# A new order of all queues for the first nine tiles of a fused quantized product and LoRA kernel

## The chip, the cores and the metric

The kernel runs on one core of a Trainium2 chip. The metric is the time of one execution on the device, in microseconds (us). A core has four compute engines with a queue of instructions each, worked off in order: TensorE (PE; its weight loads are shown apart as PEld), VectorE (DVE), ScalarE (ACT) and GpSimd (POOL). A fifth queue, SP, only issues DMAs here. Engines wait for each other by semaphores; an instruction that waits holds up all behind it in its queue.

## What is computed

x has 2 batches of 1024 rows of 2048 numbers, ctx 2 batches of 2048 x 2048. Cut to what matters:

```python
def fake_quant(x, scale, zp):
    q = clip(round(x / scale + zp), 0, 255)
    return (q - zp) * scale

# first stage
x = x + tanh(g_xattn) * (fake_quant(layernorm(x)) @ fake_quant(ctx))
# second stage, on h = layernorm(x)
logits = h @ Wr.T                        # 4 experts
gates = softmax(top 2 of logits)         # 0 for the others
mid = einsum('tf,erf->ter', h, A)        # rank 16
delta = sum_e gates_e * (mid_e @ B_e.T) * 4
out = x + tanh(g_ffn) * delta
```

## The kernel before

**Tiles and stages.** The 2048 rows of x are 16 tiles (b) of 128 rows; tiles 0 to 7 belong to batch 0, tiles 8 to 15 to batch 1. A tile lies in one of five buffers (`xr`, RING = 5), where x1, the delta and the output are made in place: tile 5 can be loaded only when tile 0 is stored. ctx is cut into 64 "rows" (i) of 128 x 1024 fp32, 0.52 MB each; 0 to 31 are batch 0 (16 blocks k of its left half, then 16 of its right half), 32 to 63 batch 1. A row is loaded to a staging place, scaled to bytes by ACT (`scale_row`, line 446), and made an fp16 code in `q2` by DVE (`code_row`, line 1139). Two byte buffers stand between the two.

**The first stage of tile b**: `stats_x` in two halves, `var_x`, `power_x` on POOL (line 376), `scale_of_x`, then ACT's `scale_x` (452), 8 transposes of PE (`turn_q1`, 654), and the copy to `q1T` (`copy_q1T`, DVE for tiles 0 and 1, ACT after, 460). The product is 4 column blocks n x 16 blocks k of 128x512 matmuls (671). For tiles 0 to 3 it is issued by halves and k, as the rows come (`rows(b, half, first, end)`, two matmuls for each k); from tile 4 on by column block (`main(b, n, first, end)`). `add_main` (DVE, 1200) adds a column block to x.

**The second stage of tile b**: `stats_h` for each column block (1205), `var_h`, `power_h` on POOL (381), `bias_h`; ACT's `high_part` (470, fp16 part of the normalized row) and `normal_half` (476, the fp32 value, by halves); POOL's `low_part` (390, their difference, two instructions for each half). PE turns the parts, 8 transposes for each half (`turn_hi` 708, `turn_lo` 715), ACT and DVE copy them out (`copy_hiT` 482, `copy_loT` 487 on ACT for half 0, 1223 on DVE for half 1), PE multiplies them with A (`mid_hi` 727, `mid_lo` 735, 8 matmuls each). DVE ranks the gates (`rank_gates`), ACT takes `gate_exp` (491), DVE `weigh` (last instruction 1257), PE `turn_gate` (746), DVE `split_gate` (1265, 1267), PE `delta` (754, 756, two matmuls for each of 4 column blocks), DVE `add_delta` (1273), SP `store`.

**The order.** Each engine's block is a list of such steps, written out by hand for the first nine tiles (0 to 8); from STEADY = 9 on it is a loop that staggers the stages of neighbouring tiles. Every step waits for what it needs, for instance:

```python
def low_part(b, h):
    pool.wait_ge(h2_ready, 2 * b + h + 1)
    pool.wait_ge(h_hi_ready, b + 1)
    wait(pool, lo_turned, 2 * (b - 1) + h + 1)
def load_x(b, h):
    wait(sp, out_stored[b % RING], 32 * (b // RING))
def turn_lo(b, h):
    pe.wait_ge(h_lo_ready, 4 * b + 2 * h + 2)
    pe.wait_ge(hiT_ready, 2 * b + h + 1)
```

Once, early, A is loaded and split (`largest_of_a`, `powers_of_a`, `copy_scales` on DVE, `scales_of_a` and `spread_scales` on PE, `split_a` on POOL, three instructions) and B likewise (`high_of_b`, `low_of_b` on DVE). `keep_busy(n)` is n matmuls whose result is not used. Rows 48 to 63 are staged in places that earlier rows leave, one of them `q1T`'s fourth buffer.

Of the kernel before, what the change touches and what calls it, by code (L numbers as in the profile page):

```python
# [34 lines left out]
def build(nc, x, ctx_in, params, lora_a, lora_b, out):  # L35
# [21 lines left out]
    with ExitStack() as stack:  # L57
# [188 lines left out]
        def _(sp):  # L246
# [34 lines left out]
            load_x(2, 0)  # L281
            load_x(2, 1)
            load_row(4)
            load_row(5)
            load_x(3, 0)
            load_x(3, 1)
            for i in range(6, 16):
                load_row(i)
            load_a()
            for i in range(16, 20):  # L290
                load_row(i)
            load_b()
            for i in range(20, 32):
                load_row(i)
            load_x(4, 0)
            load_x(4, 1)
            for i in range(32, 48):
                load_row(i)
            store(0, 0)
            load_row(48)  # L300
            store(0, 1)
            load_x(5, 0)
            load_x(5, 1)
            load_row(49)
            store(1, 0)
            load_row(50)
            load_row(51)
            store(1, 1)
            load_x(6, 0)
            load_x(6, 1)  # L310
            load_row(52)
            load_row(53)
            store(2, 0)
            store(2, 1)
            load_x(7, 0)
            load_x(7, 1)
            store(3, 0)
            load_row(54)
            store(3, 1)
            load_row(55)  # L320
            load_row(56)
            load_x(8, 0)
            load_x(8, 1)
            load_row(57)
            store(4, 0)
            load_row(58)
            store(4, 1)
            load_row(59)
            load_x(9, 0)
            load_x(9, 1)  # L330
            load_row(60)
            load_row(61)
            load_row(62)
            store(5, 0)
            load_row(63)
            store(5, 1)
            load_x(10, 0)
            load_x(10, 1)
            store(6, 0)
            store(6, 1)  # L340
# [18 lines left out]
        def _(pool):  # L359
# [54 lines left out]
            low_part(4, 0)  # L414
            power_x(6)
            low_part(4, 1)
            power_h(5)
            power_x(7)
            low_part(5, 0)
            low_part(5, 1)  # L420
            power_x(8)
            power_x(9)
            for b in range(6, 8):
                power_h(b)
                low_part(b, 0)
                low_part(b, 1)
# [10 lines left out]
        def _(act):  # L437
# [55 lines left out]
            scale_row(0)  # L493
            scale_x(0)
            scale_row(1)
            scale_row(2)
            scale_row(3)
            scale_row(4)
            scale_x(1)
            scale_row(5)  # L500
            scale_row(6)
            scale_x(2)
            scale_row(7)
            scale_row(8)
            copy_q1T(2)
            scale_row(9)
            scale_x(3)
            scale_row(10)
            scale_row(11)
            copy_q1T(3)  # L510
            for i in range(12, 30):
                scale_row(i)
            scale_x(4)
            for i in range(30, 35):
                scale_row(i)
            copy_q1T(4)
# [54 lines left out]
            for i in range(50, 56):  # L571
                scale_row(i)
# [1034 lines left out]
```

## Time and profile before

| | us |
|---|---|
| median of 3 runs (lowest, highest) | 376.11 (375.16, 376.32) |
| profiled execution, its own time | 376.49 |
| its span | 374.7 |
| PE busy | 337.6 (90%) |
| DVE busy | 290.2 (77%) |
| ACT busy | 251.0 (67%) |
| POOL busy | 96.8 (26%) |
| mean granted clock of PE | 0.982 |

The span runs from the first to the last instruction of the profiled execution; the run's own time has 1.8 us more around it. A row of the timeline names start, duration, engine, line and operation, output<-input and the number of instructions merged in it; in brackets stand the idle time before it and what ended that. A matmul is listed for longer than it holds up the next one, so starts, not durations, tell PE's pace. The granted clock is the share of 2.4 GHz that PE got; it is either 1.00 or 0.50 (1.2 GHz), and a mean between them is a mixture.

### The profile page before, as it was taken

The page shows a single profiled execution, that of the slowest core. Times are in us where ns is not written, and L with a number is a line of the kernel's source. Part 1 is how long each engine was busy: PE and PEld are TensorE (multiplying, and loading weights), DVE is VectorE, ACT ScalarE, POOL GpSimd, SP SyncE. Part 2 cuts the span into 40 slices and gives each one's busy share as a digit, 9 for nine tenths or more (in the row PEclk, how much of TensorE's full clock was granted, in tenths as well). Part 3 has the DMA queues.
Part 4 walks back from the last instruction along what each step waited for, and adds up shares of the span by engine and source line. Part 5 has one row for each costly group of instructions (what it writes and reads, how often), then busy time and mean ns, then how long its engine had stood idle before and what let it go on. Part 6 is the DMA issues. An engine that isn't in the chain of part 4 may idle for free. (4 is left out here: it accounts for less than half of the span.)

```text
span 374.7 us, 6441 instructions
## 1 busy us (share of the span) xinstructions
PE 337.6 (90%) x2372; PEld 188.7 (50%) x2372; DVE 290.2 (77%) x715; ACT 251.0 (67%) x207; POOL 96.8 (26%) x107
## 2 busy tenths in 40 slices
PE   0579989999985789999989999999999999999984
PEld 0234434445653665455555556464656565555552
DVE  4785889589996799999947796968686877866685
ACT  1769848949999699689898147464747473756150
POOL 3100430005545322033043222140505050505000
PEclk9999999999998599999999999999999999999999
DMA  7999999960046769672570524141405020202023
GB/s 218 415 420 419 420 420 420 417 278 2 3 148 239 268 247 359 213 260 87 172 258 1 193 107 152 56 170 57 170 34 192 2 115 1 114 0 114 0 86 140
DMA packets 19185, 69.17 MB, mean 185 GB/s; under 512 B 2256, under 2 KB 2256, under 8 KB 19024
## 3 DMA queue, kind: packets, MB, share of 16 engines
q1 hardware_dynamic: 19152, 68.73, 48.4%
q8 instruction: 21, 0.34, 0.4%
q14 instruction: 12, 0.10, 0.1%
HBM read 51.94 MB, written 16.78 MB: 183 GB/s over the span
## 5 line engine op out<-in xcount | busy, mean ns | idle before, releaser
L671 PE MATMUL ps_main<-q,q1T 128*128 128x512 f16 x832 | 197.4, 379 | 2.2 <-ACT q1T L460 1.6
L671 PEld LDWEIGHTS ps_main<-q,q1T 128*128 128x128 f16 x832 | 77.4, 98 | 87.2 <-issue 9.0
L446 ACT ACTIVATE c_code<-q,small_tile 128x1024 uint8<-128x1024 f32 x62 | 74.7, 1239 | 25.0 <-DVE q L1139 13.7
L470 ACT ACTIVATE h_parts<-xr,small_tile 128x2048 f16<-128x2048 f32 x15 | 31.4, 2094 | 39.4 <-DVE small_tile L1217 39.4
L390 POOL TENSOR_TENSOR h_parts<-work,h_parts 128x512 f16<-128x512 f32 x30 | 34.8, 1180 | 66.3 <-ACT work L476 66.3
L1139 DVE TENSOR_SCALAR q<-c_code,small_tile 128x1024 f16<-128x1024 f16 x64 | 37.0, 580 | 14.0 <-ACT c_code L446 13.6
L1200 DVE SCALAR_TENSOR_TENSOR xr<-ps_main,small_tile,xr 128x512 f32<-128x512 f32 x52 | 38.6, 743 | 8.1 <-PE ps_main L671 8.0
L1144 DVE BATCH_NORM_STATS2 small_tile<-xr 128x6 f32<-128x512 f32 x64 | 40.9, 680 | 5.2 <-DMA xr<-in_x 5.2
L1205 DVE BATCH_NORM_STATS2 small_tile<-xr 128x6 f32<-128x512 f32 x64 | 43.6, 687 | 0.9
L1273 DVE TENSOR_TENSOR xr<-ps_delta,xr 128x512 f32<-128x512 f32 x62 | 41.2, 680 | 3.9 <-PE ps_delta L756 3.2
L381 POOL TENSOR_TENSOR small_tile<-small_tile 128x1 f32<-128x1 f32 x16 | 9.3, 583 | 128.3 <-DVE small_tile L1213 128.3
L482 ACT COPY hT<-ps_turn 128x1024 f16<-128x1024 f16 x32 | 31.4, 1006 | 12.5 <-PE ps_turn L708 12.4
L452 ACT ACTIVATE x_byte<-xr,small_tile 128x2048 uint8<-128x2048 f32 x16 | 33.5, 2092 | 7.8 <-DVE small_tile L1159 7.8
L390 POOL TENSOR_TENSOR h_parts<-q1T,h_parts 128x512 f16<-128x512 f32 x30 | 34.1, 1160 | 1.3 <-ACT q1T L476 1.3
L754 PE MATMUL ps_delta<-lora_bT,gT_hi 128*128 128x512 f32 x60 | 30.1, 502 | 0.4 <-DVE gT_hi L1265 0.3
L460 ACT ACTIVATE q1T<-ps_gate,small_tile 128x2048 f16<-128x2048 uint8 x12 | 23.6, 1964 | 8.0 <-PE ps_gate L654 8.0
L756 PE MATMUL ps_delta<-lora_bT,gT_lo 128*128 128x512 f32 x60 | 24.4, 406 | 0.0
L642 PE MATMUL ps_main<-ident_h 128*128 128x512 f16 x47 | 12.9, 421 | 12.2 <-issue 12.2
L376 POOL TENSOR_TENSOR small_tile<-small_tile 128x1 f32<-128x1 f32 x16 | 9.5, 595 | 53.7 <-DVE small_tile L1151 53.7
L1223 DVE COPY hT<-ps_turn 128x1024 f16<-128x1024 f16 x16 | 11.0, 687 | 15.4 <-PE ps_turn L715 15.4
L671 PE MATMUL ps_turn<-q,q1T 128*128 128x512 f16 x64 | 18.1, 380 | 4.8 <-DVE q L1139 3.1
L727 PE MATMUL ps_mid<-a_parts,hT 128*128 128x136 f16 x256 | 20.8, 229 | 0.9 <-ACT hT L482 0.9
(122 smaller groups left out, 415.1 us busy)
## 6 DMA issues: line engine op xcount, KB each, us to landing
q<-in_ctx SPq DMA_DIRECT2D x62, 512.0 KB, 10.9
xr<-in_x SPq DMA_DIRECT2D x32, 512.0 KB, 4.9
out_x<-xr SPq DMA_DIRECT2D x30, 512.0 KB, 3.4
h_parts<-in_B SPq DMA_DIRECT2D x1, 1024.0 KB, 16.5
q1T<-in_ctx SPq DMA_DIRECT2D x2, 512.0 KB, 6.4
out_x<-xr SPq DMA_DIRECT2D x4, 256.0 KB, 2.3
xr<-in_A SPq DMA_DIRECT2D x1, 544.0 KB, 16.2
small_tile<-in_params SPq DMA_DIRECT2D x1, 3.0 KB, 2.6
```

The source lines that it names most:

```text
L390: nc.gpsimd.tensor_tensor(h_lo[:, half(h)][:, part], work[h][:, part], h_hi[:, half(h)][:, part], ALU.subtract).then_inc(h_lo_ready, 1)
L446: nc.scalar.activation(c_byte[:, i % 2, :], stage(i), ACT.Identity, bias=par[:, 3:4], scale=inv_s[:, 1:2]).then_inc(row_scaled, 1)
L452: nc.scalar.activation(x_byte[:, :], xr[:, b % RING, :], ACT.Identity, bias=q_scale[:, 1:2], scale=q_scale[:, 0:1]).then_inc(x_scaled, 1)
L470: nc.scalar.activation(h_hi[:, :], xr[:, b % RING, :], ACT.Identity, bias=h_bias[:, b % 2:b % 2 + 1], scale=h_rstd[:, b % 2:b % 2 + 1]).th ...
L482: nc.scalar.copy(hT[:, h, :, :], as16(ps_turn[h], F16).rearrange("p (k m) -> p k m", m=P)).then_inc(hiT_ready, 1)
L671: mm = pe.matmul(product_bank(b, n)[:, :], q1T_of(b)[:, k, :], q2[:, batch(b), k, cols(n)], start=(k == 0), stop=(k == KT - 1))
L754: pe.matmul(ps_delta[n % 2][:, :], gT_hi[:, :], lora_bT[:, cols(n)], start=True, stop=False)
L1139: nc.vector.tensor_scalar(q2[:, batch_of, k, half(h)], c_code[:, i % 2, :], low_centre[:, :], None, ALU.add).then_inc(row_coded, 1)
L1144: nc.vector.bn_stats(x_stats[:, n, :], xr[:, b % RING, cols(n)]).then_inc(x_stats_done, 1)
L1200: nc.vector.scalar_tensor_tensor(out=x1, in0=product_bank(b, n)[:, :], scalar=gain[:, 0:1], in1=x1, op0=ALU.mult, op1=ALU.add).then_inc(x1 ...
L1205: nc.vector.bn_stats(h_stats[:, b % 2, n, :], xr[:, b % RING, cols(n)]).then_inc(h_stats_done, 1)
L1273: nc.vector.tensor_tensor(x1, src[:, :], x1, ALU.add).then_inc(out_ready, 1)
```

## The change

All five lists for tiles 0 to 8 are written in another order; the loop from tile 9 on stays, and so do all steps: none is added, removed or altered. Only `rows` and `main` calls are cut at other k.

- **PE:** the halves of tiles 0 to 3 are mixed more finely: the right half (`rows(b, 1, ...)`) of tiles 0 and 1 starts before the left half of tile 3 ends. `turn_q1(1)` and `turn_q1(2)` come earlier against tile 0's products, `keep_busy(8)` stands behind `turn_q1(2)`. The second stage of tile 0 starts within tile 3's products, and the steps of tiles 1 to 3 are spread over tiles 4 and 5.
- **DVE:** `high_of_b` moves from behind row 13 to behind row 15 and `add_main(0, 0)`, `low_of_b` from behind row 14 to behind row 25; `largest_of_a` stands behind row 8; `stats_x(3)` behind row 9; rows 63 and 62 come later.
- **ACT:** `scale_x(4)` moves from behind row 29 to behind row 35, `copy_q1T(4)` behind `copy_hiT(0, 0)`, `copy_q1T(5)` behind `copy_hiT(3, 1)`.
- **POOL:** `power_x(5)` moves from behind `low_part(3, ...)` to ahead of it; `power_h(1)` behind `low_part(0, ...)`.
- **SP:** rows 5 to 9 are loaded before tile 3's x, A between its halves, B behind row 17 instead of 19; rows and stores from 47 on are mixed otherwise: `store(2, 1)` before `store(2, 0)`, `store(5, 1)` and `store(6, 0)` before `store(5, 0)`.

From the diff, the place between tile 4's last products and tile 5's first on PE, and POOL's list:

```diff
             power_h(0)
-            for b in range(1, 5):
+            low_part(0, 0)
+            low_part(0, 1)
+            power_h(1)
+            for b in range(2, 4):
                 power_h(b)
                 low_part(b - 1, 0)
                 low_part(b - 1, 1)
-            power_x(5)
...
+            for b in range(5, 7):
+                power_x(b)
+                low_part(b - 2, 0)
+                low_part(b - 2, 1)
+                power_h(b - 1)
...
-                mid_hi(3, 1)
-                turn_lo(3, 1)
-                delta(2, 0)
-                delta(2, 1)
...
+                main(4, 3, general, 9, 11)
                 delta(1, 3)
-                turn_hi(3, 0)
-                mid_lo(2, 1)
-                turn_hi(3, 1)
+                main(4, 3, general, 11, 12)
                 turn_lo(3, 0)
+                main(4, 3, general, 12, 16)
                 turn_gate(2, 5)
```

**PE, between tile 1's last deltas and tile 5's first product.** `ps_main<-q,q1T` (L671) is a product, `ps_turn<-ident_h,h_parts` a turn of a high (L708) or low (L715) part, `ps_mid` a mid_hi (L727) or mid_lo (L735), L746 a turn_gate, `ps_delta` a delta (L754 and L756). Before:

```order
479 L754 MATMUL ps_delta<-lora_bT,gT_hi 128x512
480 L756 MATMUL ps_delta<-lora_bT,gT_lo 128x512
481 L708 MATMUL ps_turn<-ident_h,h_parts 128x128 x8
482 L735 MATMUL ps_mid<-a_parts,hT 128x68 x8
483 L708 MATMUL ps_turn<-ident_h,h_parts 128x128 x8
484 L715 MATMUL ps_turn<-ident_h,h_parts 128x128 x8
485 L746 MATMUL ps_gate<-ident_f,gated 128x128
486 L727 MATMUL ps_mid<-a_parts,hT 128x136 x16
487 L715 MATMUL ps_turn<-ident_h,h_parts 128x128 x8
```

and after, where tile 3's parts are turned:

```order
477 L708 MATMUL ps_turn<-ident_h,h_parts 128x128 x8
478 L671 MATMUL ps_main<-q,q1T 128x512
479 L754 MATMUL ps_delta<-lora_bT,gT_hi 128x512
480 L756 MATMUL ps_delta<-lora_bT,gT_lo 128x512
481 L671 MATMUL ps_main<-q,q1T 128x512 x2
482 L708 MATMUL ps_turn<-ident_h,h_parts 128x128 x8
483 L735 MATMUL ps_mid<-a_parts,hT 128x68 x8
484 L671 MATMUL ps_main<-q,q1T 128x512 x2
485 L754 MATMUL ps_delta<-lora_bT,gT_hi 128x512
486 L756 MATMUL ps_delta<-lora_bT,gT_lo 128x512
487 L671 MATMUL ps_main<-q,q1T 128x512
488 L715 MATMUL ps_turn<-ident_h,h_parts 128x128 x8
```

Between the same short steps there now stand products of tile 4's last column block.

**POOL, around tile 3's low part.** L376 is a power_x, L381 a power_h (L374 and L379 in the changed file), L390 a low_part (L388). Before:

```order
28 L390 TENSOR_TENSOR h_parts<-q1T,h_parts 128x512 x2
29 L381 TENSOR_TENSOR small_tile<-small_tile 128x1
30 L390 TENSOR_TENSOR h_parts<-work,h_parts 128x512 x2
31 L390 TENSOR_TENSOR h_parts<-q1T,h_parts 128x512 x2
32 L376 TENSOR_TENSOR small_tile<-small_tile 128x1
```

After:

```order
28 L388 TENSOR_TENSOR h_parts<-q1T,h_parts 128x512 x2
29 L374 TENSOR_TENSOR small_tile<-small_tile 128x1
30 L388 TENSOR_TENSOR h_parts<-work,h_parts 128x512 x2
31 L388 TENSOR_TENSOR h_parts<-q1T,h_parts 128x512 x2
32 L379 TENSOR_TENSOR small_tile<-small_tile 128x1
```

power_x(5), row 32 before, is row 29 now, ahead of low_part(3, 0), row 30.

## Rows read from the trace of the kernel before

**Rows 1.** The page, part 1: busy us (share of the span) and instructions.
```profile
PE 337.6 (90%) x2372; PEld 188.7 (50%) x2372; DVE 290.2 (77%) x715; ACT 251.0 (67%) x207; POOL 96.8 (26%) x107
```

**Rows 2.** Stretches of the span; columns as in its first line.
```profile
core 0: us, PE busy (x) PEld busy (x) DVE busy (x) ACT busy (x) POOL busy (x), PEclk, DMA share, GB/s
12.00:86.60 74.60, 67.54 (x326) 29.97 (x326) 58.64 (x106) 56.62 (x43) 10.00 (x8) 1.00 0.95 388
86.60:108.00 21.40, 21.18 (x199) 13.40 (x200) 19.97 (x49) 21.40 (x21) 11.26 (x11) 1.00 0.04 15
108.00:118.00 10.00, 8.20 (x79) 5.28 (x76) 7.75 (x25) 10.00 (x10) 5.42 (x5) 1.00 0.69 205
118.00:137.00 19.00, 11.47 (x101) 9.58 (x102) 15.51 (x49) 15.28 (x15) 5.22 (x5) 0.64 0.76 292
137.00:216.00 79.00, 77.62 (x563) 43.43 (x562) 65.15 (x170) 62.83 (x53) 22.23 (x23) 1.00 0.55 193
216.00:374.70 158.70, 151.56 (x1112) 87.04 (x1109) 117.66 (x296) 81.65 (x67) 38.99 (x42) 1.00 0.23 88
```

**Rows 3.** Timeline of PE, 86 to 137: start, duration, engine, line, operation.
```profile
86.61 0.61 PE L671 MATMUL ps_main<-q,q1T 128*128 128x512 f16 x2 [0.63 <-DVE xr L1200]
...
87.95 2.54 PE L671 MATMUL ps_main<-q,q1T 128*128 128x512 f16 x11
90.32 0.64 PE L727 MATMUL ps_mid<-a_parts,hT 128*128 128x136 f16 x8
90.80 1.03 PE L671 MATMUL ps_main<-q,q1T 128*128 128x512 f16 x4
...
107.39 0.41 PE L735 MATMUL ps_mid<-a_parts,hT 128*128 128x68 f16 x8
107.64 1.06 PE L708 MATMUL ps_turn<-ident_h,h_parts 128*128 128x128 f16 x16
108.53 2.10 PE L671 MATMUL ps_main<-q,q1T 128*128 128x512 f16 x9
...
136.29 1.24 PE L671 MATMUL ps_main<-q,q1T 128*128 128x512 f16 x5 [1.26 <-ACT q1T L460]
```

**Rows 4.** PE's waits, 80 to 140: total us, times, longest.
```profile
PE ps_mid L735 <- DVE hT L1223: 3.8, 1, 3.8
PE ps_gate L746 <- DVE gated L1257: 2.5, 1, 2.5
```

**Rows 5.** Timeline of PE, two rows in tile 7.
```profile
181.12 1.04 PE L671 MATMUL ps_main<-q,q1T 128*128 128x512 f16 x4
...
182.47 0.82 PE L671 MATMUL ps_main<-q,q1T 128*128 128x512 f16 x3
```

**Rows 6.** Timeline of PE, where it waits for row 14's code.
```profile
50.09 0.61 PE L671 MATMUL ps_turn<-q,q1T 128*128 128x512 f16 x2 [1.66 <-DVE q L1139]
```

**Rows 7.** Timeline of DVE: row 14's code.
```profile
47.56 2.48 DVE L1139 TENSOR_SCALAR q<-c_code,small_tile 128x1024 f16<-128x1024 f16 x1
```

**Rows 8.** Timeline of DVE, 102 to 120.
```profile
102.74 1.48 DVE L1139 TENSOR_SCALAR q<-c_code,small_tile 128x1024 f16<-128x1024 f16 x1 [0.37 <-ACT c_code L446]
104.15 0.68 DVE L1273 TENSOR_TENSOR xr<-ps_delta,xr 128x512 f32<-128x512 f32 x1
104.75 0.47 DVE L1139 TENSOR_SCALAR q<-c_code,small_tile 128x1024 f16<-128x1024 f16 x1
...
119.25 1.28 DVE L1144 BATCH_NORM_STATS2 small_tile<-xr 128x6 f32<-128x512 f32 x2 [3.16 <-DMA xr<-in_x]
```

**Rows 9.** Timeline of the DMA queue SP: issues.
```profile
108.42 0.34 SPq L270 DMA_DIRECT2D out_x<-xr  x1
114.05 0.81 SPq L251 DMA_DIRECT2D xr<-in_x  x2
```

**Rows 10.** Timeline of POOL: half a low part.
```profile
119.63 2.27 POOL L390 TENSOR_TENSOR h_parts<-work,h_parts 128x512 f16<-128x512 f32 x2 [4.45 <-ACT work L476]
```

**Rows 11.** Groups of DVE, 80 to 216: count, busy us, mean ns, idle before.
```profile
L1139 DVE TENSOR_SCALAR q<-c_code,small_tile 128x1024 f16<-128x1024 f16 x31 | 17.7, 569 | 6.3 <-ACT c_code L446 6.2
```

More of the change, by code:

```diff
@@ L1337, in _ @@
-            stats_x(4, 1)
-            code_row(26)
-            var_x(4)
-            code_row(27)
-            scale_of_x(4)
-            for i in range(28, 33):
-                code_row(i)
+            code_row(33)
             add_main(0, 2)
+            stats_h(0, 2)
             add_main(0, 3)
-            stats_h(0, 2)
+            code_row(34)
+            stats_h(0, 3)
+            var_h(0)
+            stats_h(1, 0)
+            bias_h(0)
             add_main(1, 2)
-            stats_h(0, 3)
+            stats_h(1, 1)
@@ L1378, in _ @@
             var_h(3)
-            rank_gates(0)
-            code_row(37)
+            add_delta(0, 0)
+            bias_h(2)
+            add_delta(0, 1)
+            code_row(38)
+            add_delta(0, 2)
+            add_main(4, 0)
+            add_delta(0, 3)
+            copy_loT(1)
+            code_row(39)
+            bias_h(3)
+            code_row(40)
+            rank_gates(1)
+            stats_h(4, 0)
+            weigh(1)
             add_main(4, 1)
-            weigh(0)
-            stats_h(4, 0)
+            code_row(41)
@@ L1461, in _ @@
+            code_row(53)
             var_h(5)
-            add_delta(4, 3)
-            code_row(53)
             add_main(6, 0)
             bias_h(5)
+            rank_gates(4)
+            add_main(6, 1)
+            var_x(7)
             code_row(54)
-            var_x(7)
+            weigh(4)
+            scale_of_x(7)
+            stats_x(8, 0)
+            split_gate(4)
+            add_main(6, 2)
+            stats_x(8, 1)
+            stats_h(6, 0)
+            var_x(8)
+            add_delta(4, 0)
@@ L1478, in _ @@
+            copy_loT(5)
+            bias_h(6)
+            code_row(57)
+            code_row(58)
+            add_main(7, 0)
+            rank_gates(5)
+            add_main(7, 1)
+            weigh(5)
+            code_row(59)
+            split_gate(5)
             stats_x(9, 0)
-            stats_h(6, 2)
-            scale_of_x(8)
-            copy_loT(5)
             stats_x(9, 1)
-            code_row(57)
-            rank_gates(5)
-            add_main(6, 3)
+            add_main(7, 2)
@@ L1486, in _ @@
+            stats_h(7, 0)
             var_x(9)
-            weigh(5)
-            code_row(58)
-            stats_h(6, 3)
-            split_gate(5)
-            add_main(7, 0)
-            code_row(59)
-            var_h(6)
             add_delta(5, 0)
+            stats_h(7, 1)
+            scale_of_x(9)
             code_row(60)
+            add_main(7, 3)
+            stats_h(7, 2)
+            code_row(61)
+            stats_h(7, 3)
+            var_h(7)
+            copy_loT(6)
+            bias_h(7)
@@ L1508, in _ @@
-            code_row(63)
-            copy_loT(6)
-            add_main(7, 3)
-            stats_h(7, 3)
-            rank_gates(6)
-            var_h(7)
-            bias_h(7)
-            weigh(6)
-            add_main(8, 0)
-            stats_h(8, 0)
-            split_gate(6)
             add_delta(6, 0)
             add_delta(6, 1)
+            stats_h(8, 1)
             add_delta(6, 2)
-            add_main(8, 1)
-            add_delta(6, 3)
-            stats_h(8, 1)
             copy_loT(7)
+            code_row(63)
```

786 lines of the change are left out of this document (390 added, 396 removed).

## The prediction

> **What bounds the kernel now.** I first read the page's shares: TensorE (PE) is busy for 337.6 of 374.7 us and no other engine passes 77%, so PE's queue sets the time, and the question is where PE loses [rows 1]. The stretches, read next, put numbers on that [rows 2]. At about 216.0 PE comes to tile 9's first product, and from there the program is unchanged, so what follows is taken as a block of 158.7 us. Ahead of it PE is idle for 7.1 us of 12 to 86.6, for 0.2 us of 86.6 to 108, for 1.8 us of 108 to 118, for 7.5 us of 118 to 137 (where the granted clock averages 0.64), and for 1.4 us of 137 to 216.
>
> The timeline shows what stands in the gap [rows 3]. Tile 4's product begins at 86.61, its last 9 matmuls start at 108.53, and the first matmul of tile 5's starts at 136.29. Between them PE has nothing but short steps of the second stage of tiles 1 to 4, and each depends on an answer from ScalarE (ACT), VectorE (DVE) or GpSimd (POOL). The list of waits names the two longest: 3.8 us for DVE's copy of the turned low part and 2.5 us for the gate weights [rows 4]. After PE had been idle for 3.8 us, matmuls ran at the 1.2 GHz level: a mean of 0.64 over 19 us is 13.7 us at that level.
>
> **The method.** No instruction is added or taken away, the 25 warming matmuls included, so PE's work to tile 9 is the same and only waits and the clock can move. From pieces that run without a wait I take PE's steps, as the distance to the next start: 0.216 us for a product matmul (87.95 to 90.32 is 11), 0.45 for 8 transposes (107.64 to 108.53 is 16), 0.47 for a mid_hi, 0.25 for a mid_lo [rows 3], 0.47 for a delta of two matmuls (181.12 to 182.47 is four products and one, 0.49; others were 0.47) [rows 5], and an estimated 0.13 for a turn_gate, a single matmul. I add them along the new order and ask at each wait whether the thing waited for is there.
>
> **Part A, the first half tiles.** Before, the tightest row was row 14: PE reached it, without waiting, at 27.9 us of its own work, and waited until 50.1 [rows 6], a lag of 22.1 us behind its work. The row was late since high_of_b stands ahead of it on DVE, up to 47.56, and since it was coded beside POOL's split_a, in 2.48 us [rows 7] where one undisturbed takes 0.47 [rows 8]. The new order puts high_of_b and low_of_b behind rows 15 and 25, but calls rows 14 and 15 at 21.0 and 22.7 us of work. Walked through: q1T(1) is made behind row 6, x tile 2 is coded for turn_q1(2) at about 27.2, the 8 warming matmuls end at 29.4, which is a lag of 19.6, and spread_scales ends near 39. Then rows 14 and 15 are coded beside split_a, by 41.5 and 44.0 at 2.2 and 2.5 us each: a lag of 21.3 at row 15. That is 0.8 less than 22.1, and the wait of 0.6 us for a free bank at tile 4 [rows 3] goes, as add_main(3,2) falls 0.8 us ahead of its reader. Sum 1.4; I count **1.0**. The order of the loads costs nothing: rows 5 to 9 come one to two places earlier, x tile 3 and A later, and at 388 GB/s or more [rows 2] a place of 0.52 MB is at most 1.35 us; row 31 still lands near 60 and PE calls it at 69.
>
> **Part B, tile 4's start to tile 5's start.** Before: 86.61 to 136.29, 49.7 us [rows 3]. By the steps above its work is 34.2 us (64 product matmuls 13.8, 19 groups of 8 transposes 8.6, 8 mid_hi 3.8, 8 mid_lo 2.0, 12 deltas 5.6, 3 gates 0.4), so 15.5 us are waits, half clock and the fills behind each wait. In the new order PE has 66.0 us of work to tile 4's first product, which at a lag of 21.3 is 87.3, and 30.0 us from there to tile 5's (the same 64 products and 12 deltas, but 13 groups of transposes, 6 mid_hi and 6 mid_lo). In it the steps of tile 0 stand in tile 3's products, and those of tiles 2 and 3 in tile 4's and 5's. Only nine short groups, 3.9 us, are left between tile 4's last product matmul and tile 5's first. I find three waits there:
> - turn_hi(3,0) meets high_part(3), which ACT ends 0.6 us late.
> - turn_lo(3,0) needs POOL's low_part(3,0), and POOL now has power_x(5) ahead of it. That chain starts at DVE's add_delta(0,3): PE's turn_gate(0) comes at 92.2, and from there DVE has split_gate, stats_h, var_h, add_delta, bias_h, add_delta, a code row, add_delta, add_main and add_delta, 5.1 us at the steps of its rows (0.60 us from start to start for one over 512 columns, 0.39 for a code row [rows 8]), so with a wait or two it ends near 97.6. Then the store, 5.6 us until the buffer's load is issued, as 108.42 to 114.05 before, and 5.2 us to the statistics, as 114.05 to 119.25 [rows 8, 9]. That gives 108.4; with stats_x, code rows, copy_loT, stats_x and var_x on DVE 112.6, power_x 0.6 and low_part 2.27 [rows 10] 115.5. PE comes near 113.1: 2.2 us, and 2.5 us more for PE if that load lands that much later.
> - copy_hiT(3,1) stands behind scale_x(5) and a row on ACT: 0.3 us.
>
> These are 3.1 us, plus 0.5 for fills: tile 5 starts at 87.3 + 30.0 + 3.6 = 120.9. None reaches the 3.8 us pause behind which the clock fell. So B gives 15.5 - 3.6 = **11.9**.
>
> **Part C, tiles 5 to 8.** Before PE idles 1.4 us here. Walked on with PE at a lag of 24.4, the tightest meetings are scale_x(7), 1 us ahead of turn_q1(7), code_row(62), 0.9 us ahead of its matmul, and rank_gates(7), whose weights come 1.0 us ahead of turn_gate(7). Stores and loads on SP: x tile 8 waits behind row 57 and lands at about the time DVE asks, x tile 9 some 0.8 us late, x tile 10 (behind store(5,1), store(6,0) and store(5,0)) near 204, as the loop asks for it; DVE absorbs these. C gives **1.0**.
>
> **What eats some of it.** After 80 us DVE's 31 code rows take a mean of 569 ns [rows 11], where an undisturbed one takes 470 [rows 8]: 3.1 us of stretching that my walk, at 470, leaves out. Most is covered, since in the walk DVE waits for PE for some 4.5 us between tiles 5 and 9, so I take **0.4**; its bounds are 0 and 3.1 (nothing covered).
>
> Sum: 1.0 + 11.9 + 1.0 - 0.4 = 13.5. The profiled execution took 376.49 us (span 374.7 and 1.8 around it), so 363.0; the median of the runs lies 0.4 lower, so **362.6 us**.
>
> **A rule weighed.** From 86.6 to 108 PE ran 199 matmuls, 80 of them transposes, among products, as the new order does everywhere, and the granted clock was 1.00 [rows 2]; 8 of them took 0.45 us [rows 3]. The Trainium skill (TensorE: Matmul & The Clock Gate, Part 4) has it that transposes don't count as work that holds the clock up. By that rule the clock could fall where steps are spread, and the sum would be that of the second rival; this trace, with 40% of transposes at a clock of 1.00, does not bear it out.
>
> **The rivals.**
> 1. *The gap is only moved, 12%.* From 86.6 to 108 ACT is busy for all of 21.4 us and DVE for 20.0 [rows 2], and the new order asks them for the same work in 13 us less. If at each of tiles 5 to 9 PE waits 1.2 us for ACT's or DVE's lateness, 6 us come back: 369. For it: margins of 1 us. Against: from 137 to 216 DVE is busy for 65 of 79 us, so it can catch up.
> 2. *The clock falls once more, 5%.* PE now waits up to 2.5 us for turn_q1(2) near 25 us, right after warming, and 1.9 us before that. A stretch of 13.7 us at 1.2 GHz, as before, costs 6.9 us under full load: 369.5. The same price holds if the fall comes among the spread transposes. Against: before, the clock stayed up through every wait but that of 3.8 us [rows 2, 4].
> 3. *Slower, 4%: the code rows meet POOL.* Rows 36 to 63 are 28 rows. If each falls beside a low_part and takes 1.48 us [rows 8], DVE has 28.3 us more; less the 3.1 that it had before and the 4.5 us of slack, PE is 20.7 us later: 383. The Trainium skill (GPSIMD Engine Reference, Specifications) says that this engine shares its SBUF interfaces with VectorE and contends with its instructions in a two-port mode; the rows agree, with 2.48 us at worst [rows 7]. It turns the sign once 18 rows are hit (18 x 1.01 = 13.5 + 4.5). Against: their mean was 569 ns [rows 11], and POOL's 16 low parts of 2.27 us fill a third of the stretch.
> 4. *Nothing changes, 2%:* the spread steps free no time as main(5,0) waits for q1T(5) anyway: copy_q1T(5) would have to end at 136 instead of 121. Its chain hangs on the same load of x tile 5, which starts with add_delta(0,3), 10 us earlier; against it. 376.
>
> **How the numbers follow.** The forecast as worked out has 77%. Within it the bounds are A from -2 (turn_q1(2) later) to +2, the load of x tile 5 from 2.2 us better to 5 us worse, stretching 0 to 3.1. All together would give 358 to 372; the ends that are likely together are 360 and 367. Rivals 1 and 2 lie at 369, and the range reaches to them: **359.5 to 369.5**, with rivals 3, 4 and the far corners outside. Differences over 0.3% (1.1 us) count as a change, about what a measurement of this kernel can tell. Faster 0.94, same 0.02, slower 0.04.
>
> **What would show it.** Tile 4's first product at 87 to 89 and tile 5's at 121 (118 to 124); no granted clock below 1.00 between 17 and 340 us; DVE's wait for x tile 5 near 108; tile 9's first product at 202 to 203. If tile 5 starts by 122 and tile 9 only after 207, rival 1 is right. A granted clock of 0.5 after 17 us is rival 2. Code rows at a mean above 0.8 us are rival 3. If tile 5's first product waits for q1T beyond 130, rival 4. The prediction is wrong if any stretch of PE's idle time above 3 us is left between 52 and 200.

## The result, and the profile after

The changed kernel takes 359.43 us (median of 4 runs, 358.62 to 361.46) beside 376.22 us of the kernel before (4 runs, 375.16 to 376.65): a ratio of 0.956, with a 95% interval of 0.952 to 0.960. It is faster by 16.8 us where 13.5 were forecast. The profiled execution took 361.46 us, the slowest of the four, beside 376.49 before: 15.0 us less. Two executions among the experiments below, one of e1 (896.73 us) and one of e9 (367.23 us), were slow runs and stand outside all medians and ratios. PE's share of the span rose from 90% to 93% [rows 1]:

```profile
PE 333.1 (93%) x2372; PEld 186.3 (52%) x2372; DVE 287.8 (80%) x715; ACT 251.9 (70%) x207; POOL 95.3 (26%) x107
```

The stretches, cut at tile 4's and 5's first products and where PE came close to tile 9's (us, then for each engine busy us and instructions, the granted clock, DMA share, GB/s):

```profile
12.00:87.80 75.80, 71.27 (x375) 33.64 (x376) 64.67 (x118) 66.84 (x51) 15.21 (x14) 0.98 0.92 376
87.80:108.00 20.20, 20.20 (x188) 12.94 (x186) 17.76 (x53) 19.48 (x20) 9.63 (x9) 1.00 0.35 131
108.00:118.00 10.00, 7.40 (x79) 4.81 (x77) 9.51 (x31) 9.79 (x9) 5.03 (x5) 1.00 0.46 160
118.00:121.30 3.30, 3.30 (x33) 2.59 (x33) 2.97 (x7) 3.30 (x4) 0.48 (x1) 1.00 0.82 223
121.30:201.10 79.80, 79.42 (x598) 45.36 (x598) 69.39 (x189) 66.91 (x56) 22.26 (x24) 1.00 0.59 207
201.10:359.70 158.60, 151.49 (x1111) 86.95 (x1109) 117.73 (x296) 81.67 (x67) 39.01 (x42) 1.00 0.28 101
```

From tile 9 on nothing changed, 158.6 us beside 158.7 [rows 2]. The stretch that held 7.5 us of idle time and 13.7 us at 1.2 GHz is gone: what PE still waits for between 108 and 118 is 2.6 us. PE's timeline there, the rows that answer to [rows 3] and [rows 4]:

```profile
87.79 0.38 PE L671 MATMUL ps_main<-q,q1T 128*128 128x512 f16 x1
...
110.50 0.62 PE L708 MATMUL ps_turn<-ident_h,h_parts 128*128 128x128 f16 x8 [0.82 <-ACT h_parts L470]
...
115.54 0.62 PE L715 MATMUL ps_turn<-ident_h,h_parts 128*128 128x128 f16 x8 [1.46 <-POOL h_parts L388]
...
117.93 0.61 PE L654 MATMUL ps_gate<-ident_h,x_byte 128*128 128x128 f16 x8 [0.33 <-DVE gT_lo L1279]
...
121.28 1.89 PE L671 MATMUL ps_main<-q,q1T 128*128 128x512 f16 x8
```

Tile 4's first product is at 87.8, tile 5's at 121.3, and what is left between them is 33.5 us where it was 49.7. The waits are those at turn_hi(3,0), turn_lo(3,0) and, a small one, at turn_q1(5). But the clock did fall once, early. PE's rows:

```profile
24.66 0.61 PE L671 MATMUL ps_turn<-q,q1T 128*128 128x512 f16 x2 [0.56 <-DVE q L1151]
27.36 0.62 PE L654 MATMUL ps_delta<-ident_h,x_byte 128*128 128x128 f16 x8 [2.09 <-ACT x_byte L452]
...
30.88 0.63 PE L671 MATMUL ps_mid<-q,q1T 128*128 128x512 f16 x1
```

and the stretches there:

```profile
22.50:28.50 6.00, 3.36 (x21) 1.33 (x19) 4.50 (x10) 6.00 (x6) 0.72 (x1) 0.97 1.03 421
28.50:31.40 2.90, 2.90 (x9) 0.99 (x7) 2.71 (x3) 2.90 (x2) 0.00 (x0) 0.50 1.01 410
31.60:50.00 18.40, 18.40 (x94) 8.76 (x93) 14.13 (x25) 14.57 (x11) 6.57 (x4) 1.00 1.03 420
```

Behind the wait of 2.09 us for turn_q1(2), PE ran 3.4 us (28.2 to 31.6, by the record of the granted clock) at the 1.2 GHz level.

**How the runs are compared.** For each profile I take the start of tile 4's, tile 5's and tile 9's first product, and the lag: that start less PE's own work ahead of it, which is every matmul before it at the prediction's steps. A lag grows by idle time and by time at half clock alike. The work is 64.0, 98.0 and 175.1 us in the order of before, 66.7, 96.6 and 175.1 in that of after (the prediction's walk had 66.0 for the 66.7). The filler of e4 is not counted as work. All experiments are in one table; each median stands in front of that of the kernel before on the same chip. Its median is between 375.3 and 376.2 us from chip to chip, so times of two profiles are compared only roughly, and gains in time are given by the ratios.

| kernel | median (before) | profiled | tile 4 / 5 / 9 start | lag at 4 / 5 / 9 |
|---|---|---|---|---|
| before | 376.2 | 376.5 | 86.6 / 136.3 / 216.1 | 22.6 / 38.3 / 41.0 |
| after | 359.4 (376.2) | 361.5 | 87.8 / 121.3 / 201.1 | 21.1 / 24.7 / 26.0 |
| e1 early lists only | 372.1 (375.6) | 371.4 | 84.1 / 131.3 / 211.0 | 20.1 / 33.3 / 35.9 |
| e2 late lists only | 368.9 (375.6) | 369.7 | 96.2 / 129.7 / 209.2 | 29.6 / 33.1 / 34.1 |
| e3 bunched | 365.7 (375.6) | 363.6 | 86.0 / 124.0 / 203.1 | 19.4 / 27.5 / 28.0 |
| e4 filler in before | 374.8 (375.6) | 373.7 | 86.8 / 134.3 / 213.3 | 22.8 / 36.3 / 38.2 |
| e5 one DVE step moved in before | 375.2 (375.3) | 375.3 | 86.6 / 134.8 / 214.9 | 22.6 / 36.8 / 39.8 |
| e6 warming ahead | 358.3 (375.3) | 358.2 | 85.2 / 118.6 / 197.9 | 18.5 / 22.0 / 22.8 |
| e7 power_x(5) behind | 364.2 (375.3) | 365.6 | 87.7 / 125.7 / 205.2 | 21.1 / 29.1 / 30.2 |
| e8 ACT forward | 362.7 (375.3) | 362.8 | 86.1 / 122.8 / 202.4 | 19.5 / 26.2 / 27.3 |
| e9 after again | 360.5 (375.4) | 362.0 | 87.7 / 121.2 / 201.6 | 21.0 / 24.6 / 26.5 |
| e10 e6 again | 358.9 (375.4) | 358.9 | 85.1 / 118.6 / 198.4 | 18.5 / 22.1 / 23.3 |
| e11 combined | 360.0 (375.4) | 359.9 | 85.9 / 119.1 / 199.4 | 19.2 / 22.5 / 24.3 |

### The profile page after: what moved, and what is told of

It is laid out like the page before. It is cut to its first block and busy times, and to the rows that moved or that the text cites. A ratio compares the mean times of both kernels' runs of the same rounds, so it can differ in the third digit from the quotient of the medians.

```text
span 359.7 us, 6441 instructions
## 1 busy us (share of the span) xinstructions
PE 333.1 (93%) x2372; PEld 186.3 (52%) x2372; DVE 287.8 (80%) x715; ACT 251.9 (70%) x207; POOL 95.3 (26%) x107
## 5 line engine op out<-in xcount | busy, mean ns | idle before, releaser
L671 PE MATMUL ps_main<-q,q1T 128*128 128x512 f16 x832 | 200.5, 379 | 0.0
L671 PEld LDWEIGHTS ps_main<-q,q1T 128*128 128x128 f16 x832 | 76.8, 98 | 82.7 <-issue 8.2
L446 ACT ACTIVATE c_code<-q,small_tile 128x1024 uint8<-128x1024 f32 x62 | 74.8, 1237 | 13.5 <-DMA q<-in_ctx 7.9
L388 POOL TENSOR_TENSOR h_parts<-work,h_parts 128x512 f16<-128x512 f32 x30 | 34.3, 1166 | 46.0 <-ACT work L476 46.0
L379 POOL TENSOR_TENSOR small_tile<-small_tile 128x1 f32<-128x1 f32 x16 | 8.9, 559 | 117.3 <-DVE small_tile L1225 117.3
L1151 DVE TENSOR_SCALAR q<-c_code,small_tile 128x1024 f16<-128x1024 f16 x64 | 33.2, 524 | 4.9 <-ACT c_code L446 4.5
L388 POOL TENSOR_TENSOR h_parts<-q1T,h_parts 128x512 f16<-128x512 f32 x30 | 34.1, 1159 | 5.4 <-ACT q1T L476 5.4
L754 PE MATMUL ps_delta<-lora_bT,gT_hi 128*128 128x512 f32 x60 | 30.1, 502 | 0.4 <-DVE xr L1285 0.3
L374 POOL TENSOR_TENSOR small_tile<-small_tile 128x1 f32<-128x1 f32 x16 | 9.7, 604 | 73.2 <-DVE small_tile L1163 73.2
L642 PE MATMUL ps_main<-ident_h 128*128 128x512 f16 x47 | 14.7, 467 | 12.3 <-issue 12.3
L756 PE MATMUL ps_delta<-lora_bT,gT_lo 128*128 128x512 f32 x60 | 23.8, 397 | 0.0
L715 PE MATMUL ps_turn<-ident_h,h_parts 128*128 128x128 f16 x256 | 19.5, 219 | 1.5 <-POOL h_parts L388 1.5
L727 PE MATMUL ps_mid<-a_parts,hT 128*128 128x136 f16 x256 | 20.5, 223 | 0.0
```

The lines of the kernel that those rows point to most:

```text
L388: nc.gpsimd.tensor_tensor(h_lo[:, half(h)][:, part], work[h][:, part], h_hi[:, half(h)][:, part], ALU.subtract).then_inc(h_lo_ready, 1)
L446: nc.scalar.activation(c_byte[:, i % 2, :], stage(i), ACT.Identity, bias=par[:, 3:4], scale=inv_s[:, 1:2]).then_inc(row_scaled, 1)
L671: mm = pe.matmul(product_bank(b, n)[:, :], q1T_of(b)[:, k, :], q2[:, batch(b), k, cols(n)], start=(k == 0), stop=(k == KT - 1))
L754: pe.matmul(ps_delta[n % 2][:, :], gT_hi[:, :], lora_bT[:, cols(n)], start=True, stop=False)
L1151: nc.vector.tensor_scalar(q2[:, batch_of, k, half(h)], c_code[:, i % 2, :], low_centre[:, :], None, ALU.add).then_inc(row_coded, 1)
```

## The experiments

**Do the parts add up? e1 and e2.** The lists are cut where the second stage starts: e1 takes everything ahead of it in the new order and the rest in the old, e2 the reverse. On PE, e1 ends its new part so (against the changed kernel):

```diff
                 rows(3, 1, 4, 6, general)
-                rows(2, 1, 11, 13, general)
-                turn_hi(0, 0)
-                rows(2, 1, 13, 14, general)
+                rows(2, 1, 11, 15, general)
+                rows(3, 1, 6, 7, general)
...
+                turn_q1(4, 0)
+                rows(3, 1, 9, 16, general)
+                main(4, 0, general, 0, 2)
+                turn_hi(0, 0)
```

> The lists of the changed kernel up to the start of the second stage (on PE up to turn_hi(0,0), on DVE up to var_h(0), on ACT up to scale_x(4), on SP up to the first store, on POOL up to power_h(0)), and from there the remaining steps in the order of the kernel before. Theory (the terms add up): only part A's gain, 1.5 us, shows: tile 4's first product near 85.1, the gap behind it stays, 374.7 us beside 376.2. Rival (the gap takes back what comes earlier, since tile 5's load and its answers do not move with PE): within 0.5 us of before, tile 5's first product at 136 again.

> The reverse: the lists of before up to the start of the second stage, then the remaining steps in the order of the changed kernel. Theory: parts B and C show alone, 13.4 us: 362.8 us, tile 5's first product 33.5 us behind tile 4's, no stretch at half clock behind 88 us. Rival: the late part needs the early one, because ACT is busy without a pause from 86 us on and now starts further behind; then PE waits in tile 4 by 2 us or more beyond the changed kernel's 3.6, and the time is above 364.5 us.

e1 gave 372.09 us, ratio 0.990 (0.987 to 0.993); e2 368.94, ratio 0.981 (0.977 to 0.985). By the ratios e1 wins 3.7 us and e2 7.1, together 10.8 of the changed kernel's 16.5. In e1 tile 4 starts earlier than forecast (lag 20.1), and the old middle costs less than in the kernel before: 13.2 us of lag beside 15.7. Its granted clock is at 0.50 for 6.8 us there instead of 13.7; why is not shown. e2 is slower than the 364.5 us above which the rival lay, but not by the rival's way: the waits come ahead of tile 4's product and not in it. From 12 us to that product PE idles 10.4 us beside 4.5 in the changed kernel, and from there to tile 5's 2.6 us in both. Its gap from tile 4 to tile 5 is 33.5 us like the changed kernel's, but tile 4 starts 8.4 us later. PE of e2:

```profile
86.00 0.62 PE L777 MATMUL ps_turn<-ident_h,h_parts 128*128 128x128 f16 x8 [3.46 <-ACT h_parts L516]
```

and where it came from, DVE's add_main(0,2) and (0,3), in e2 and then in the changed kernel:

```profile
77.19 1.41 DVE L1283 SCALAR_TENSOR_TENSOR xr<-ps_turn,small_tile,xr 128x512 f32<-128x512 f32 x2 [1.03 <-PE ps_turn L740]
```
```profile
70.86 0.75 DVE L1212 SCALAR_TENSOR_TENSOR xr<-ps_turn,small_tile,xr 128x512 f32<-128x512 f32 x1
...
72.26 0.73 DVE L1212 SCALAR_TENSOR_TENSOR xr<-ps_turn,small_tile,xr 128x512 f32<-128x512 f32 x1
```

Without the finely mixed halves tile 0's product is done 5.6 us later (78.6 beside 73.0). The new middle calls turn_hi(0,0) ahead of tile 4's product, PE stands 3.5 us for it, and the granted clock is 0.50 from 86.9 to 93.7. So some 5.7 us are won only when both parts are there: the first finishes tile 0 early enough for the second to spread steps over tile 3's products.

**Is it the spreading? e3.**

```diff
-                main(4, 2, general, 4, 15)
+                main(4, 2, general, 4, 16)
                 turn_gate(1, 5)
+                main(4, 3, general)
                 turn_hi(2, 1)
                 turn_lo(2, 0)
-                main(4, 2, general, 15, 16)
                 delta(1, 0)
                 delta(1, 1)
                 mid_hi(2, 0)
-                main(4, 3, general, 0, 2)
                 turn_lo(2, 1)
-                main(4, 3, general, 2, 4)
...
```

> The changed kernel, but tile 4's last column block, 16 products of 0.216 us, stands in one piece ahead of the short steps of tiles 1 to 3 between which it was spread; all other queues are as changed. Theory (the spreading on PE is what pays): the answers of ACT, DVE and POOL come when they came, PE stands waiting for them where products stood, and 3.4 us and more are lost: 362.8 to 364 us, 367 or more if the clock falls in a wait. Rival (what pays is the order on the other queues, the earlier load of tile 5 above all): within 1 us of the changed kernel.

365.73 us, ratio 0.974 (0.970 to 0.978), beside the changed kernel's 0.956: some 7 us slower by the ratios. Its profile is its fastest run; in it, tile 5's first product is 38.0 us behind tile 4's instead of 33.5, and PE idles 5.1 us between the two instead of 2.6. PE's two longest waits:

```profile
112.18 0.62 PE L708 MATMUL ps_turn<-ident_h,h_parts 128*128 128x128 f16 x8 [1.57 <-ACT h_parts L470]
...
117.28 0.62 PE L715 MATMUL ps_turn<-ident_h,h_parts 128*128 128x128 f16 x8 [2.70 <-POOL h_parts L388]
```

and the clock fell behind the second one:

```profile
118.50:121.80 3.30, 3.30 (x20) 2.90 (x21) 2.46 (x6) 3.30 (x4) 0.96 (x1) 0.50 0.91 322
```

The theory holds, with a price between its two figures: the same 16 products stand either in the waits or in front of them. But this is 4.5 us of the gap only. With tile 4's last block in one piece the gap is still 11.7 us shorter than the 49.7 of before, and no run separates what of that is the spreading of the other steps and what the order of the other queues.

**What was half clock worth? e4.** Filler products in the two long waits of the kernel before:

```diff
                 turn_hi(3, 0)
+                pe.wait_ge(x1_ready, parts_done(4, 2))
+                keep_busy(16)
                 mid_lo(2, 1)
                 turn_hi(3, 1)
                 turn_lo(3, 0)
+                keep_busy(9)
                 turn_gate(2, 5)
```

> The kernel before with 25 more products of no use: 16 ahead of mid_lo(2,1), where PE waited 3.8 us, and 9 ahead of turn_gate(2), where it waited 2.5 us. They fill the waits, no answer comes sooner. Theory (of the 15.5 us of part B some 4.4 were half clock between 117 and 133 us): the granted clock stays at 1.00 and 2.2 us are won, as tile 5's byte copy is ready at 131.2 us and PE's turn_q1(5) stood at 133.5: 374.0 us. Rival: the clock falls all the same, or the chain of tile 5 sets the end whatever PE's clock: within 0.7 us of before, or slower by the filler that does not fit.

The granted clock is 1.00 from 86 to 137, tile 5 starts 2.0 us earlier (134.3). The medians differ by 0.8 us, a ratio of 0.9987 (0.9968 to 1.0006), which isn't told from no change. The interval leaves at most 1.2 us of the whole time. So the fall of 13.7 us cost about 2 us at tile 5 and less at the end: at full clock PE meets the next answers earlier and waits for them:

```profile
132.17 1.07 PE L708 MATMUL ps_turn<-ident_h,h_parts 128*128 128x128 f16 x16 [1.15 <-ACT h_parts L470]
134.30 1.24 PE L671 MATMUL ps_main<-q,q1T 128*128 128x512 f16 x5 [1.06 <-ACT q1T L460]
```

**Was the 3.8 us wait only DVE's order? e5.** In the kernel before DVE stood 3.16 us for tile 5's load [rows 8] with copy_loT(2) behind it, for which PE waited.

```diff
             bias_h(4)
-            stats_x(5, 0)
             add_delta(1, 2)
             copy_loT(2)
             add_delta(1, 3)
+            stats_x(5, 0)
```

> The kernel before with one step of DVE moved: stats_x(5,0), which stood at 119.25 us behind a wait of 3.2 us for the load of x, now comes behind add_delta(1,2), copy_loT(2) and add_delta(1,3). Theory (PE's wait of 3.8 us was that load's, because copy_loT(2) was queued behind it): mid_lo(2,1) starts near 117.9 instead of 121.8; next PE waits some 3 us for POOL's low_part(3,0), ended at 121.9; turn_gate(2) comes near 124.4 instead of 126.6, and 2 to 5 us are won (the more if the clock stays up): 371 to 374 us. Rival (the load of x tile 5 sets the gap's end by itself): tile 5's first product stays within 1 us of 136, and so does the time of 375.6.

375.23 us beside 375.27, no difference. The wait went (the row of mid_lo(2,1) has none), and the next one took its place:

```profile
117.78 0.41 PE L735 MATMUL ps_mid<-a_parts,hT 128*128 128x68 f16 x8
118.03 0.61 PE L708 MATMUL ps_turn<-ident_h,h_parts 128*128 128x128 f16 x8
121.93 1.04 PE L715 MATMUL ps_turn<-ident_h,h_parts 128*128 128x128 f16 x8 [3.30 <-POOL h_parts L390]
125.36 0.48 PE L746 MATMUL ps_gate<-ident_f,gated 128*128 128x128 f32 x1 [2.38 <-DVE gated L1257]
```

The clock fell within the 3.30 us, at 120.7. Tile 5 starts 1.5 us earlier, less than the theory's 2 to 5 and more than the rival's 1; the time is the one that the rival gave. In a chain in which three engines answer in turn, one wait less only uncovers the next.

**What held tile 4's lag? e6.**

```diff
                 rows(0, 0, 2, 7, general)
-                turn_q1(2, 0)
                 keep_busy(8)
+                turn_q1(2, 0)
                 rows(1, 0, 0, 5, general)
```

> The changed kernel with its 8 warming products ahead of turn_q1(2) instead of behind it, so that they fill PE's wait of 1.1 to 2.1 us for that tile's bytes. Theory (this wait and the warming behind it set the lag until tile 4): tile 4's first product comes 1.7 us sooner than in the changed kernel, at 84.3 to 86.1 us by whether the early stretch at half clock falls on work or on a wait: 357.8 us. Rival (the codes of rows 9 to 15 set it, as the prediction had it): within 0.6 us of the changed kernel.

358.26 us (358.15 to 358.44), ratio 0.954 (0.952 to 0.957). PE now fills the wait:

```profile
26.07 1.89 PE L642 MATMUL ps_main<-ident_h 128*128 128x512 f16 x8
27.80 0.61 PE L654 MATMUL ps_delta<-ident_h,x_byte 128*128 128x128 f16 x8
28.25 0.38 PE L671 MATMUL ps_mid<-q,q1T 128*128 128x512 f16 x1
```

Tile 4's lag is 18.5 us, where e3 and e8, which have the changed kernel's early lists, have 19.4 with the clock's fall at nearly the same place (19.9 and 19.4 us). That is 1 us, not 1.7.

**Who is late at turn_lo(3,0)? e7.**

```diff
-            for b in range(5, 7):
-                power_x(b)
-                low_part(b - 2, 0)
-                low_part(b - 2, 1)
-                power_h(b - 1)
+            low_part(3, 0)
+            low_part(3, 1)
+            power_x(5)
+            power_h(4)
...
```

> The changed kernel with POOL's power_x(5) behind low_part(3,0) and low_part(3,1) again, as before the change. The prediction put PE's wait at turn_lo(3,0) on this move. Theory (it is ACT that is late: normal_half(3,0) ends at 112.7, when power_x(5)'s input comes too): the wait of 1.5 us shrinks by 0.5 us alone, and scale_x(5) comes 4 us later, so tile 5's first product waits for q1T(5) and the time grows by 3 to 4 us: 362 to 363.5. Rival (as the prediction had it): the wait of 1.5 us goes and little comes in its place, 358 to 359.5.

364.19 us, ratio 0.970 (0.967 to 0.972). The wait at turn_lo(3,0) shrank from 1.46 to 1.04 us, and another came that I had not named. DVE, then PE:

```profile
117.78 0.21 DVE L1171 TENSOR_SCALAR small_tile<-small_tile 128x1 f32<-128x1 f32 x1 [3.27 <-POOL small_tile L374]
```
```profile
119.99 0.33 PE L749 MATMUL ps_gate<-ident_f,gated 128*128 128x128 f32 x1 [3.45 <-DVE gated L1272]
```

DVE's scale_of_x(5) waits for the late power_x(5), and weigh(2) is queued behind it; PE waits for that, and the clock is at 0.50 from 120.2 to 123.7. The theory's cause for the wait (ACT) holds; the price, 4.5 us in the gap, came by another way than the one expected. Moving power_x(5) forward was right. The rows of ACT and POOL in the changed kernel show it:

```profile
110.34 1.24 ACT L446 ACTIVATE c_code<-q,small_tile 128x1024 uint8<-128x1024 f32 x1
111.47 1.24 ACT L476 ACTIVATE work<-xr,small_tile 128x1024 f32<-128x1024 f32 x1
```
```profile
112.69 0.56 POOL L374 TENSOR_TENSOR small_tile<-small_tile 128x1 f32<-128x1 f32 x1 [5.94 <-DVE small_tile L1163]
113.21 2.27 POOL L388 TENSOR_TENSOR h_parts<-work,h_parts 128x512 f16<-128x512 f32 x2
```

ACT writes what low_part(3,0) reads only at 112.7, behind a code row, so power_x(5) delays it by 0.5 us and no more.

**Can ACT's steps go forward? e8.**

```diff
             copy_hiT(2, 1)
-            scale_row(43)
             copy_loT(2)
             high_part(3)
-            scale_row(44)
             normal_half(3, 0)
+            scale_row(43)
             copy_hiT(3, 0)
             normal_half(3, 1)
             gate_exp(2)
+            scale_row(44)
             scale_x(5)
-            scale_row(45)
             copy_hiT(3, 1)
             copy_q1T(5)
+            scale_row(45)
...
-            code_row(42)
             copy_loT(2)
-            code_row(43)
             stats_x(5, 1)
             var_x(5)
+            code_row(42)
+            code_row(43)
```

> The changed kernel with ACT's steps for tile 3 ahead of its code rows: scale_row(43) and (44) behind normal_half(3,0) and further, scale_row(45) behind copy_q1T(5); POOL's low_part(3,0) ahead of power_x(5); on DVE stats_x(5,1) and var_x(5) ahead of rows 42 and 43, copy_loT(3) ahead of row 45. Theory (ACT, busy without a pause from 86 to 121 us, sets PE's last waits in tile 4): the waits at turn_hi(3,0), 0.8, and turn_lo(3,0), 1.5, go, up to 1 us comes back at turn_gate(2), and tile 5's first product is 1.3 us closer to tile 4's than the 33.5 us of the changed kernel: 358.1 us. Rival (the chain of tile 5's load sets tile 5's start, with no margin): within 0.4 us of the changed kernel.

362.69 us, ratio 0.966 (0.961 to 0.970), slower than the changed kernel: both theories fall. The wait at turn_lo(3,0) is gone and that at turn_hi(3,0) is 0.69, but PE then waits in one piece:

```profile
116.68 0.33 PE L749 MATMUL ps_gate<-ident_f,gated 128*128 128x128 f32 x1 [2.82 <-DVE gated L1272]
```

and runs at 0.50 from 118.4 to 121.8. DVE was late by its two code rows, which now ran beside POOL's low_part (109.86, 2.46 us) and took 1.27 us each instead of 0.47:

```profile
110.06 2.54 DVE L1154 TENSOR_SCALAR q<-c_code,small_tile 128x1024 f16<-128x1024 f16 x2
```

This is the third rival's mechanism at the size of two rows. The Trainium skill (GPSIMD Engine Reference, Specifications) has it that POOL shares its SBUF interfaces with VectorE; the row agrees.

**The changed kernel again, and a mended combination: e9 to e11.** e10's kernel is e6's. e11 joins e6 and e8, and moves DVE's answers ahead of its rows (shown against e8):

```diff
             var_x(5)
-            code_row(42)
-            code_row(43)
             add_delta(1, 2)
             rank_gates(2)
+            code_row(42)
             scale_of_x(5)
-            add_delta(1, 3)
             weigh(2)
+            add_delta(1, 3)
...
-                turn_q1(5, 3)
                 delta(2, 0)
                 delta(2, 1)
+                turn_q1(5, 3)
```

> The changed kernel itself once more, as the measure for the other two of this set. It gives 359.4 us again beside 376.2 us of before (ratio 0.955). In the runs so far with the new early lists the granted clock fell once, for 3.4 us, near 19 or near 28 us. Theory (only the fall near 28 us hits work; the other hits a wait): where it falls near 28 us tile 4 starts 1.7 us later, at 87.8, where it falls near 19 us or not at all at 86.1. Rival: the early part varies for another reason.

> The kernel of the sixth run (8 warming products ahead of turn_q1(2)) once more, beside the changed kernel on the same chip. Theory: 1.0 us faster than the changed kernel, as tile 4's lag was 18.5 us beside 19.4 where the clock fell near 19 us in both, and less spread between its runs. Rival: no difference, within 0.4 us.

> The kernel of the eighth run mended: ACT's steps for tile 3 ahead of its code rows and low_part(3,0) ahead of power_x(5) as there, but on DVE weigh(2) directly behind scale_of_x(5), rows 42 to 45 behind what PE waits for, on PE delta(2,0) and (2,1) ahead of turn_q1(5), and the 8 warming products ahead of turn_q1(2). Theory (in the eighth run the waits of 2.3 us only met in one of 2.8 us at turn_gate(2), behind two code rows of 1.27 us each beside POOL, and the clock fell; with the gate's weights 2 us sooner the wait is below 1 us): tile 5's first product 32.1 us behind tile 4's instead of 33.5, no half clock behind 52 us, 357.0 us. Rival (the answers of ACT and POOL for tile 5 only move the wait on, to turn_q1(5) or q1T(5)): as the sixth run's kernel or slower.

e9: 360.47 us, ratio 0.9593 (0.9569 to 0.9616), a little above the 0.955 forecast. Its profile has the fall at 28.3 us and tile 4 at 87.7, as in the changed kernel's and e7's. So with the same early lists there are three profiles with the fall near 28.2 us and a lag of 21.0 to 21.1 (after, e7, e9), and two with it near 19.4 us and a lag of 19.4 (e3, e8); e1 has it there too, and 20.1 by a wait of 0.6 us of its own at tile 4's first product. In those two PE waits 2.2 us for q1T(0) and has warming products around it, so the slow stretch hits little that counts; near 28 us it hits the warming behind turn_q1(2) and the first rows. In both kinds turn_q1(2) starts near 27.3 us; what the slow stretch costs before it only shortens the wait there (1.1 and 1.2 us in e3 and e8, 2.1 in the others). What decides between the two places is not shown.

e10: 358.87 us, ratio 0.9557 (0.9532 to 0.9583), 1.6 us faster than e9 on the same chip; the intervals of the ratios overlap in 0.9569 to 0.9583. Its lag at tile 4 is 18.5 as in e6. Two profiles and both ratios say the same, so I take it for the best kernel here, by 1 to 2 us, though the overlap leaves a smaller difference possible. Less spread between its runs is not shown: 2.1 us beside 2.5. Three of its five executions had a mean granted clock of 1.00 and took 358.17 to 360.27 us, the two others (0.995 and 0.994) 358.87 and 358.65: in this order the early fall costs nothing that shows.

e11: 359.95 us, ratio 0.959 (0.956 to 0.962). The second stage's wait did shrink to 0.89 us at turn_gate(2), no half clock is left before the end, and the gap is 33.2 us, but not the 32.1 expected; another 1.1 us is lost right behind it, and 1.7 us early:

```profile
40.84 0.61 PE L674 MATMUL ps_turn<-q,q1T 128*128 128x512 f16 x2 [1.66 <-DVE q L1154]
...
114.32 0.33 PE L749 MATMUL ps_gate<-ident_f,gated 128*128 128x128 f32 x1 [0.89 <-DVE gated L1272]
...
122.10 0.42 PE L738 MATMUL ps_mid<-a_parts,hT 128*128 128x68 f16 x8 [1.08 <-ACT hT L490]
```

The last is copy_loT(3), to which ACT now comes behind rows 44 and 45; the first is row 14's code. The rival is right: the waits move on.

## Why the prediction was right, and where its sizes were off

The direction and the mechanism held, and the size was too small: 13.5 us against 15.0 in the profiled run and 16.8 in the medians. The median, 359.43, lies 0.07 below the low end of the range. By its own steps:

- **Part A, counted at 1.0.** By the lags of the profiles 1.5 (22.6 to 21.1). The walk put tile 4's first product at 87.3 and it came at 87.8: the sum of the work was 0.7 us too small (66.7 and not 66.0 by its own steps), and the lag 0.2 us smaller than walked (21.1 for 21.3). The step behind it was wrong twice, in opposite directions. Row 15 was to set the lag; rows 14 and 15 took 3.10 us together, not 2.2 and 2.5, and PE met row 14 without a wait:

```profile
41.21 3.10 DVE L1151 TENSOR_SCALAR q<-c_code,small_tile 128x1024 f16<-128x1024 f16 x2
```

  And the warming was walked at full clock, while in this profile it ran at half. Where the fall comes at 19 us, as in e3 and e8, the lag is 19.4, a gain of 3.2 us. That may be a part of the 1.8 us between the profiled gain and the medians' one; no unprofiled run shows where its clock fell.
- **Part B, counted at 11.9.** 12.1 by the lags (15.7 to 3.6); the gap was put at 33.6 us and is 33.5. The waits were 0.82 (forecast 0.6) at turn_hi(3,0) and 1.46 (2.2) at turn_lo(3,0); none at copy_hiT(3,1) (0.3), but 0.33 at turn_q1(5). The chain of tile 5's load ran much as walked: power_x(5) done at 113.2, low_part(3,0) at 115.5. DVE's wait for that load near 108 did not come, as the load was issued at 102.1 and 103.0, some 3.6 us behind the store and not 5.6. The cause given for turn_lo(3,0), power_x(5) ahead on POOL, was wrong for two thirds: e7 gives 0.4 us to it and 1.0 to ACT.
- **Half clock inside B.** The prediction took waits and half clock as one sum, so its size did not rest on a split. e4 shows that taking away half clock alone is worth about 2 us at most, e5 that taking away the longest wait alone is worth 1.5. 4.5 of the 12.1 us hang on the products of tile 4's last block between the steps (e3). The late lists alone bring the gap of 33.5 us, but then 8.5 us of lag come ahead of tile 4 (e2: 29.6 beside 21.1), so B also needs the early end of tile 0. How the other 7.6 us divide between spread steps and the other queues stays open.
- **Part C, 1.0, and the stretching, -0.4.** Mis-sized: 1.3 net where 0.6 stood (2.7 to 1.35 between tiles 5 and 9). PE's idle time fell from 1.4 to 0.4 us, and code rows were stretched less and not more: a mean of 501 ns for 29 (0.9 us over 470) beside 569 for 31 [rows 11]:

```profile
L1151 DVE TENSOR_SCALAR q<-c_code,small_tile 128x1024 f16<-128x1024 f16 x29 | 14.4, 501 | 0.1
```

- **Tile 9** came at 201.1, not 202 to 203. The sum was too small by 1.5 us there: 0.5 in A, 0.2 in B, 0.7 to 0.8 in C with the stretching.
- **The rivals.** The first did not come: the margins of 1 us held, and PE's only listed wait from 121 to 201 us is 0.33 us (at a delta, 159.25). The second did in kind, 3.4 us at half clock behind the wait for turn_q1(2), at a price of 1.7 us and not 6.9; "no granted clock below 1.00 between 17 and 340 us" was wrong. The third is real for a code row beside low_part (e8) but hit too few rows here. The fourth is out: q1T(5) was there at 121.1.
- **The rule weighed.** The prediction counted 80 transposes of 199 matmuls from 86.6 to 108 us; the trace has 71, 36% and not 40%, and only 55 of the 199 are products. With transposes spread among products everywhere, the granted clock was 1.00 in every stretch from 31.6 to 201 us. By the rule of the Trainium skill (TensorE: Matmul & The Clock Gate, Part 4) it could have fallen there; this trace does not show it. From 80 us on the clock fell within waits of 3.8 us (before), 3.3 (e5) and 1.30 (e1, the second of two, behind one of 1.83), and up to 1.7 us behind waits of 3.46 (e2), 3.45 (e7), 2.82 (e8) and 2.70 (e3); not at the 1.46 of the changed kernel. So the pause of 3.8 us, which the prediction took as its measure, was none: in the kernel before the fall came at 119.1, 1.1 us into that wait, and shorter waits brought it too.

## What to carry to other kernels

Where short dependent steps stand in one piece, count the independent work that could stand between them, and first ask which earlier order makes their inputs ready in time: by the ratios the two parts of this change alone won 3.7 and 7.1 us, both together 16.5. Removing one wait or the slow clock alone won nothing measurable (e4, e5), and where small waits gathered into one of 2.8 us, about 3 us were lost (e8). Here warming work in front of a wait, where it fills it, was about 1 us of lag better than behind it (e6, e10).

## What the runs showed that was not expected

- In all six profiles with the changed kernel's early lists the granted clock was 0.50 once ahead of tile 4 for 3.4 us, at one of two places 9 us apart: 19.4 us (e1, e3, e8) or 28.2 us (e7, e9 and its own). In e6 and e10 it fell near 19 to 20 us, in e11 not at all. With the place, tile 4's start moved by 1.7 us, though the order up to there was the same (e3 and e8 beside e7, e9 and its own). In e2, with the old early lists, it fell at 18.6 us; in the profiles of before, e4 and e5 not at all there.
- A wait for the gate weights came from a step that has nothing to do with them: scale_of_x(5), waiting 3.27 us for POOL, stood ahead of weigh(2) in DVE's queue (e7). Read the queue of the engine that is named, not only its instruction.
- Two code rows beside POOL's low_part took 2.54 us instead of 0.94 (e8).
